# A one-core decoder layer: calls in another order on four engines, and longer runs of products of zeros

## The reference

```python
x = x + _L0_attn_ref(_layernorm(x, axis=-1), ...)              # selective scan
x = x + _L0_xattn_ref(_layernorm(x, axis=-1), fside, ctx)      # one expert per batch, int8 rounding
x = x + _L0_ffn_ref(_layernorm(x, axis=-1), w_gate_up, w_down) # gated feed-forward, int8 rounding
```

```python
delta = jax.nn.softplus(jnp.einsum('blr,dr->bld', dt, dtproj_w) + dtproj_b)
h = dA * h + dBu        # dA = exp(delta * A), dBu = delta * Bm * u
y = jnp.einsum('bdn,bn->bd', h, c)
```

## Time and profile before

| | |
|---|---|
| median of three runs | 221.69 us (221.39 to 223.66) |
| span of the profiled execution | 221.1 us |
| the profiled execution's own time beside it | the runs' median, 0.59 us above that span |
| DVE busy | 194.2 us, 88% of the span |
| PE busy | 161.8 us, 73% |
| ACT busy | 159.4 us, 72% |
| POOL busy | 148.7 us, 67% |
| products of zeros | 148 on PE, 41.0 us busy with their overlaps |
| loads of an ACT table | 8, each 1.28 us |

### The profile page before, as it was taken

The page is one execution under the profiler, slowest core; times in us unless marked ns, Lnnn a source line. Parts: engine busy times, 40 slices in busy tenths (PEclk is TensorE's granted clock), DMA queues, the critical chain, the costliest instruction groups (busy, mean ns, idle before and its releaser), DMA issues.

```text
span 221.1 us, 3460 instructions
## 1 busy us (share of the span) xinstructions
PE 161.8 (73%) x952; PEld 111.6 (50%) x952; DVE 194.2 (88%) x401; ACT 159.4 (72%) x353; POOL 148.7 (67%) x150
## 2 busy tenths in 40 slices
PE   8379698887962865983586756667696968676789
PEld 3145385565651753753485545455564555443344
DVE  1789987999899999999989999997999979886663
ACT  3549979879799976956795757874777896773251
POOL 2510379999999899999999899886426363434000
PEclk9958999999998599999969996997999999999999
DMA  5993951854543633546333651510000000000203
GB/s 159 327 365 98 186 185 37 212 139 138 166 158 110 179 113 102 187 77 187 112 100 98 162 125 44 203 42 0 0 0 1 3 0 0 0 3 27 71 0 98
DMA packets 15109, 23.29 MB, mean 105 GB/s; under 512 B 1137, under 2 KB 6641, under 8 KB 15089
## 3 DMA queue, kind: packets, MB, share of 16 engines
q1 hardware_dynamic: 13792, 21.92, 35.0%
q10 hardware_dynamic: 1296, 1.15, 1.6%
HBM read 21.88 MB, written 1.18 MB: 104 GB/s over the span
## 4 chain that ended last, share of the span: by engine, by line
DVE 35%; PE 20%; issue 18%; ACT 15%; POOL 8%; DMA 1%; ACTq 1%; POOLq 0%; DVEq 0%
DVE hid L1108 9%; DVE hid_sb L1108 6%; DVE prod L1119 5%; POOL drive L348 4%; ACT pD L494 4%; PE pY L986 3%; PE pF L918 3%; PE pY L786 3%; DVE w L1294 2%; DVE am L1053 2%; PE pA L253 2%; POOL prod L385 2%; ACT w L591 1%; DMA x_sb<-x 1%; ACT L494 1%
## 5 line engine op out<-in xcount | busy, mean ns | idle before, releaser
L348 POOL TENSOR_TENSOR drive<-du,bc 128x512 f32<-128x512 f32 x64 | 79.9, 1277 | 4.3 <-DMA bc<-bc_dram 4.1
L494 ACT ACTIVATE pD<-delta,negA 128x255 f32<-128x255 f32 x128 | 54.9, 468 | 15.1 <-DVE hid L1108 12.8
L1108 DVE TENSOR_TENSOR_SCAN hid<-pD,drive 128x512 f32<-128x512 f32 x40 | 48.9, 1223 | 3.1 <-ACT pD L494 1.4
L786 PE MATMUL pY<-ident,prod 128*128 128x128 f32 x256 | 36.8, 294 | 14.0 <-POOL prod L385 10.7
L986 PE MATMUL pY<-zero 128*128 128x512 bf16 x148 | 41.0, 402 | 1.0 <-POOL zero L305 1.0
L786 PEld LDWEIGHTS pY<-ident,prod 128*128 128x128 f32 x256 | 31.2, 152 | 19.9 <-DVE prod L1119 10.2
L385 POOL TENSOR_TENSOR prod<-hid_sb,bc 128x512 f32<-128x512 f32 x24 | 30.5, 1278 | 2.3 <-DVE hid_sb L1108 2.2
L1108 DVE TENSOR_TENSOR_SCAN hid_sb<-pD,drive 128x512 f32<-128x512 f32 x24 | 29.0, 1207 | 0.9 <-ACT pD L494 0.9
L1119 DVE TENSOR_TENSOR prod<-hid,bc 128x512 f32<-128x512 f32 x40 | 27.1, 679 | 0.5 <-PE pY L786 0.2
L333 POOL TENSOR_TENSOR rstd<-ve,mhalf 128x2 f32<-128x2 f32 x12 | 8.6, 715 | 24.5 <-ACT ve L678 24.5
L986 PEld LDWEIGHTS pY<-zero 128*128 128x128 bf16 x148 | 14.9, 103 | 12.6 <-issue 2.7
(11 more groups left out here) (166 smaller groups left out, 328.2 us busy)
## 6 DMA issues: line engine op xcount, KB each, us to landing
bc<-bc_dram SPq DMA_DIRECT2D x32, 512.0 KB, 4.9
w<-w_gate_up SPq DMA_DIRECT2D x1, 1408.0 KB, 8.5
x_sb<-x SPq DMA_DIRECT2D x4, 256.0 KB, 3.6
fs_t<-w_in_t SPq DMA_DIRECT2D x1, 1024.0 KB, 11.8
out<-x_sb ACTq DMA_DIRECT2D x8, 128.0 KB, 2.3
w<-w_down SPq DMA_DIRECT2D x1, 704.0 KB, 9.8
ctx_t<-w_out_t SPq DMA_DIRECT2D x1, 512.0 KB, 11.7
xproj<-xproj_t SPq DMA_DIRECT2D x1, 160.0 KB, 3.0
```

What stands on the lines that cost most here:

```text
L348: pool.tensor_tensor(drive[:, s % 2, h], du[:, b, h].unsqueeze(1).to_broadcast([P, SPS, T]), bc[:, g % 4, 0].rearrange("p (n t) -> p n t", ...
L494: act.activation(decay[:, h, n, 1:T], delta[:, b, h, 1:T], ACT.Exp, scale=negA[:, h, k:k + 1]).then_inc(S["decay_ready"], 1)
L786: ins = pe.matmul(pY[:, j, h * P:(h + 1) * P], prod[:, s % 2, h, n, j * P:(j + 1) * P], ident[:], start=(s + n + h + j == 0), stop=False, ...
L1108: dve.tensor_tensor_scan(hid_sb[:, k % 2] if pooled(s, h) else hid, decay[:, h].rearrange("p n t -> p (n t)"), drive[:, s % 2, h].rearrang ...
```

## The change

The lists of calls on PE, DVE, ACT and POOL are written in a new order. The same steps are called, each once. Some pairs of semaphores become one that counts both events (`sq_ready` and `sm_ready`, `raw_pre` and `raw_ready`, `w1_scale` and `w1_rec`, `stored0` and `stored1`). `filler(k, n)` now issues `2 * n` products instead of two, and there are 304 of them instead of 148. A few lines of the diff (the tables run over some 190 lines):

```diff
-                pool.tensor_tensor(sq[:], rat[:], half[:], ALU.pow).then_inc(S["sq_ready"], 1)
-                pool.wait_ge(S["sq_ready"], b + 1)
+                pool.tensor_tensor(sq[:], rat[:], half[:], ALU.pow).then_inc(S["sm_ready"], 1)
+                pool.wait_ge(S["sm_ready"], 2 * b + 1)
...
-                act.wait_ge(S["sm_ready"], b + 1)
+                act.wait_ge(S["sm_ready"], 2 * b + 2)
...
-            def filler(k, i):
+            def filler(k, n):
...
-                for _ in range(2):
+                for _ in range(2 * n):
...
-            filler(0, 11); filler(0, 3); filler(0, 7); filler(0, 1); filler(0, 4); filler(0, 9); filler(0, 10)
+            filler(0, 14); prep_turn(0); filler(0, 9); prep_bc(0); prep_dt(0); prep_turn(1); prep_pre(0)
```

More of the change, by code:

```diff
@@ new lines, in _ @@
+            prep_conv(1); filler(0, 3); prep_dt(1); prep_bc(1); prep_pre(1); prep_turn(2); filler(0, 1)
+            prep_conv(2); sum_step(0, 0); turn_w1(0, 0); filler(1, 3); prep_bc(2); sum_step(0, 1); sum_step(0, 2)
+            turn_w1(0, 1); filler(1, 11); prep_turn(3); sum_step(0, 3); prep_dt(2); filler(1, 2); prep_pre(2)
+            sum_step(0, 4); sum_step(0, 5); prep_conv(3); turn_w1(0, 2); sum_step(0, 6); sum_step(0, 7); skip_y(0)
+            turn_w1(1, 0); turn_w1(1, 1); prep_dt(3); sum_step(1, 0); prep_pre(3); turn_w1(1, 2); filler(2, 3)
@@ L1415, in _ @@
[L1415 to L1419 removed]
+            prep_stats(0); zeros(); prep_norm(0); prep_stats(1); constants(); conv_first(); shift(0, 1)
@@ new lines, in _ @@
+            weigh(0, 4, 0); scan(0, 5, 0); scan(0, 5, 1); weigh(0, 5, 0); scan(0, 6, 0); wmax_inv(); weigh(0, 6, 0)
+            scan(0, 6, 1); scan(0, 7, 0); weigh(0, 7, 0); scan(0, 7, 1); weigh(0, 7, 1); scan(1, 0, 0)
+            weigh(1, 0, 0); scan(1, 0, 1); scan(1, 1, 0); residual1(0); weigh(1, 1, 0); scan(1, 1, 1); scan(1, 2, 0)
+            stats2(0); weigh(1, 2, 0); scan(1, 2, 1); scan(1, 3, 0); prep_bc(3); weigh(1, 3, 0); shift(1, 0)
+            scan(1, 3, 1); prep_delta(2); weigh(1, 3, 1); scan(1, 4, 0); scan(1, 4, 1); weigh(1, 4, 0)
@@ new lines, in _ @@
+            inv_w1(1); scan(3, 0, 1); weigh(3, 0, 0); residual1(2); scan(3, 1, 0); stats2(2); gate_up1(1)
+            weigh(3, 1, 0); shift(1, 2); gate1(1); scan(3, 1, 1); scan(3, 2, 0); up1(1); scan(3, 2, 1); amax_a(1)
+            weigh(3, 2, 0); ratio_a(1); scan(3, 3, 0); gate_up3(0, 0, 0); weigh(3, 3, 0); inv_smooth2(1); amax_x(2)
+            scan(3, 3, 1); max_ad(1); weigh(3, 3, 1); scale_ad(1); ratio_x(2); inv_ad(1); scan(3, 4, 0)
+            scan(3, 4, 1); weigh(3, 4, 0); inv_smooth1(2); gate_up3(0, 0, 1); scan(3, 5, 0); scan(3, 5, 1)
@@ new lines, in _ @@
+            weigh(3, 5, 0); expert_out(1); full3(0); scan(3, 6, 0); scan(3, 6, 1); stats3(1); max_x(2)
+            weigh(3, 6, 0); scale_x1(2); max_w(2); inv_x1(2); max3(1); scale_w1(2); scan(3, 7, 0); scale3(1)
+            inv_w1(2); weigh(3, 7, 0); inv3(1); gate_up3(0, 1, 0); scan(3, 7, 1); max4(0, 0); weigh(3, 7, 1)
+            gate_up1(2); gate_up3(0, 1, 1); up1(2); amax_a(2); scale4(0, 0); ratio_a(2); inv4(0, 0); residual1(3)
+            factor4(0, 0); full3(1); inv_smooth2(2); stats2(3); gate_up3(1, 0, 0); max_ad(2); scale_ad(2); norm2(3)
```

282 lines of the change are left out of this document (126 added, 156 removed), and 1 row of the table names.

## The result

The changed kernel takes 228.21 us (median; 226.81 to 228.46) against 222.68 beside it: a ratio of 1.026, interval 1.022 to 1.031. The forecast was 226.8, in a range of 219 to 231. The profiled execution has a span of 226.6 us and took 228.46.

The account below looks back on a forecast made before the run. DVE was taken to bound the kernel, so a new order could win only idle time. The stage terms sum to +5.15, a span of 226.25; with 0.59 added the forecast was 226.8 us, range 219.0 to 231.0.

Parts of the forecast that it names:

- the work that DVE owes in batches 0 and 3: DVE work moved between stages: 3.4 us from before the first scan into batch 0, 3.7 from behind the scans into batch 3.
- Prologue (-0.8): Up to the first scan: later transposition and convolution, but moved DVE work brings the scan near 26.8; -0.8 us.
- Batch 0 (+3.15): First batch of scans: added DVE and ACT work, each waiting for the other, makes the stage 33.4 us; +3.15.
- Batch 1 (+3.9): Second batch: separate table loads per logarithm make DVE wait 1.1 and 2.7 us for ACT's decays; +3.9 with a copy.
- Batch 2 (-0.7): Third batch: nearly the same order, with the wait at the later-placed expert_out(0) gone; -0.7 us.
- Batch 3 (+4.4): Last batch: 3.7 us more DVE work and waits behind a silu with loads between the last decays; +4.4.
- behind (-4.1): Experts and feed-forward after the last scan: 3.7 us of DVE work gone, 3.4 of idle time kept; -4.1.
- End (-0.7): Last stage: unmagic3(3) no longer behind store issues wins 0.95 us, a swapped gate product costs 0.25; -0.7.
- From span to time (+0.59): Whole kernel: 0.59 us added to the predicted span, as between the earlier profile's span and the median of runs.
- the clock's: Rival: 156 more products of zeros keep TensorE's clock up and cut idle time, giving 216.6 us; chance 0.14.
- Zeros in the way: Rival: runs of zero products on PE delay sums between scans, about 4 us more, 230.8; chance 0.13.
- The delays: Rival: batch 0 at its lower bound and half the logarithm wait covered leave no change, 222.3 us; chance 0.23.

Follow-up runs that it names:

- control: The changed kernel run once more without any edit: 226.70 us, ratio 1.020 to the kernel before.
- last experiment: Changed kernel with 14 leading zeros, three maxima before the first scan, old logarithm order, first silu behind the last decay, eight zeros at the first expert: 220.14 us.
- the maxima ahead: Changed kernel with two maxima of weights moved on DVE from batch 0 back ahead of the first scan: 226.20 us, ratio 1.019.

## Why the prediction was right

By stage, predicted against changed and control: 26.8 against 27.16 and 26.73; 33.4 against 32.57 and 32.76; 34.7 against 34.65 and 34.64; 34.5 against 35.61 and 33.72; 38.4 against 37.98 both; 37.0 against 37.74 and 38.33; 21.4 against 20.93 and 20.94. The sum of 226.25 met a span of 226.6. That it came so near is partly luck: the stages were missed by up to 1.1 us, in both directions, and the control's span is 225.1. What carried the forecast were the waits behind ACT in batches 1 and 3 and the work that DVE owes in batches 0 and 3. The terms, one by one:

- **Prologue (-0.8).** The size was right; the path was right in some executions and not in others. In the control the transposition starts at 9.85 us (9.2 predicted), the convolution at 11.12 (10.6), the delta at 22.27 (21.9), and DVE works without a pause from there to the first scan, at 26.73 (26.8). In the changed kernel's profile the transposition starts at 8.58 and the delta at 21.00, and what ends the stage is POOL's first drive, at 25.79 (26.13 before), behind the transfer of B and C, a term that the prediction did not have. With half the leading zeros DVE is ready 3 us early, and the first scan comes at 26.44, within the spread of the other executions. That the zeros cost what DVE could have done meanwhile, the 3.4 us that it owes, is argued and not shown: with half of them and the maxima ahead of the scan (last experiment) batch 0 still takes 32.33.
- **Batch 0 (+3.15).** Measured +2.3. DVE's busy time grew by 2.25, not by 3.4: the step of 1.10 that it owes took 0.76 there, and a copy of 0.4 (`prep_bc(3)`) left for batch 1. Its idle time stayed at 3.6 (3.3 taken). Owed work is shown for 1.1 us of the stage, by the maxima ahead; with 2.0 us of work taken out, in the last experiment, waits took the place of most of it. One reading was wrong: `prep_ln(1)` with its two loads stood between two halves of a step before, too (at 40.94 us, of step 4; now of step 3). What DVE waits behind it was 0.36 us, and is 0.59 in the changed kernel and 1.65 in the control.
- **Batch 1 (+3.9).** Measured +3.8; the waits 0.92 (1.1 predicted) and 0.92 + 1.90 (2.7). That splitting the logarithms can cost this much is shown on the kernel before (+4.0). That it is the loads alone is refuted: without the two, the stage stays, with DVE waiting at a decay that comes late behind a relu, a normalisation and a copy, and for sums that are late on PE. It took the order of three engines to win back 2.1, and 3.2 with one copy more.
- **Batch 2 (-0.7).** The wait at `expert_out(0)`, 0.69 us before, is gone as forecast. The stage was mis-sized in either direction all the same, -1.5 or +0.4: it is 33.7 where PE's clock holds at the first expert and 35.6 where it falls to 1.2 GHz for some 6 us (34.1 and 34.4 in two profiles where it is down for under 4). No term of the sum held that.
- **Batch 3 (+4.4) and behind (-4.1).** Measured +3.9 and -3.3 (-2.7 in the control). DVE's work in batch 3 grew by 3.0 (3.7 predicted), and of its 2.24 us of idle time 2.22 are the one wait behind the silu (1.3 predicted, and 0.7 for others that did not come). The cause is the silu with its loads ahead of the last decay and the centring: with it behind them, the wait is gone. Held against the 32.54 of the two other profiles made from the kernel before, the stage grew by 5.4.
- **End (-0.7).** Measured -1.1, but of that 0.8 goes in a run of the kernel before with the stores where they were, so it depends on how long the issues took in the one execution that the earlier trace rows shows. The time with the stores behind, 0.5% less, agrees with the sign.
- **From span to time (+0.59).** Mis-sized: the profiled execution took about 1.8 us more than its span, as did all the others. I had set the span of one execution against the median of others; with 1.8 the forecast would have been 228.1.

A table load takes 1.28 us, and the silu follows 0.01 us after it (158.04, 159.33): the drain that the Trainium skill adds (ScalarE: Activation LUTs, What ACT_TABLE_LOAD costs), by which the prediction's estimate of the sum would have been up to 232.3, appears behind none of the changed kernel's eleven that follow the one at the start of the program.

Of the rivals, the clock's has a true mechanism and too small a price: by the stages, the zeros between the scans earn about 2 us in batch 0 and 0.7 in batch 3, less than the new order loses. The Trainium skill (TensorE: Matmul & The Clock Gate, What's actually happening) says that activity releases the throttle, and the windows at 47.7 us agree, 0.50 without the zeros and 1.00 with them. Zeros in the way were seen in one place, once the logarithms no longer hid them; the 0.98 us at 41.45 is a wait for PE too, with six zeros ahead of the sum and the clock down. The delays were not absorbed.

## What to carry to other kernels

Cut the span at marks that each engine must pass, and compare busy time and idle time stage by stage: a stage can repeat to hundredths where the whole wanders by 2 us, and a loss that only moved shows as a stage longer and another shorter by as much. Do it on more than one execution of the kernel before as well: here one profile of it had 1.5 us in batch 3 and 0.8 at the end that the next did not have. Where one engine loads tables, what counts is not the number of loads but which consumer has no work in hand while they last; put everything that can wait behind them, on the engines fed by it too. Before work is taken off the start, look for what ends it: here a transfer of B and C that landed late left room for other work, not for an earlier start.

## What the runs showed that was not expected

- The same gap of 2.24 us on PE was followed by the lower clock in the changed kernel and not in the control; the same kernel thus differs by 1.9 us in one stage.
- How long 28 leading products of zeros take differs between executions of the same list: the transposition behind them starts between 8.58 and 10.06 us.
- Removing products that only add zeros made batch 0 longer by 2.0 us and batch 3 by 0.7; taking out only the 20 that stood in the way of a sum won 0.25 us of the stage instead of the 1.2 that the sum was waited for.
